# Attention on one core: the last weighted sums of a half issued together, and the copy of the sums two scores earlier

## The reference

```python
xn = layernorm(x)                                   # x: 8 x 1024 x 256
kqv = xn @ W_kqv.T                                  # 16 heads of 16 columns
score = einsum('bhsd,bhnd->bhsn', q, k) / 16 + slope[h] * (n - s)
attn = softmax(score, axis=-1)
out = einsum('bhsn,bhnd->bhsd', attn, v)
# routed experts: softmax of xn @ gate_w.T, the best 2 of 8, weights scaled by 2.5
y = sum over the two experts of combine * (silu(xn @ w_gate) * (xn @ w_up)) @ w_down
result = x + out + y + shared_expert(xn)
```

## Time and profile before

| | |
|---|---|
| median of three runs | 2621.71 us |
| the profiled execution | 2615.34 us |
| its span, first to last instruction | 2613.7 us |
| TensorE busy | 2438.0 us, 93% |
| VectorE busy | 1949.5 us, 75% |
| ScalarE busy | 1545.0 us, 59% |
| mean granted TensorE clock | 0.968 |

### The profile page before, as it was taken

How to read it: one execution, slowest core, us unless ns; L and a number is a source line. 1 busy time by engine, 2 the same in 40 slices (tenths; PEclk the granted TensorE clock), 3 DMA queues, 4 the chain that set the end, 5 groups by cost and what they waited for, 6 DMA issues and landing times.

```text
span 2613.7 us, 56931 instructions
## 1 busy us (share of the span) xinstructions
PE 2438.0 (93%) x19376; PEld 1487.8 (57%) x19377; DVE 1949.5 (75%) x2945; ACT 1545.0 (59%) x3215; POOL 790.3 (30%) x1004
## 2 busy tenths in 40 slices
PE   7999999963999999964999999999999999999998
PEld 5888888862999999861333333333333333333333
DVE  5666666643555555537899999999999999999994
ACT  3333333332333333320788888888888888888887
POOL 2222222235222222250101523505425135052250
PEclk9999999986999999985999999999999999999999
DMA  6999888740222222216324343534434353435330
GB/s 182 177 174 179 154 146 145 129 66 21 70 69 70 69 68 68 67 45 99 71 46 73 78 81 66 98 50 91 81 61 93 59 89 77 73 73 87 56 72 23
DMA packets 178264, 228.51 MB, mean 87 GB/s; under 512 B 43069, under 2 KB 127805, under 8 KB 178057
## 3 DMA queue, kind: packets, MB, share of 16 engines
q1 hardware_dynamic: 153336, 172.15, 36.7%
q0 software_dynamic: 22560, 50.69, 7.8%
q10 hardware_dynamic: 2176, 3.02, 0.3%
HBM read 131.60 MB, written 93.79 MB: 86 GB/s over the span
## 4 chain that ended last, share of the span: by engine, by line
PE 40%; DVE 13%; issue 1%; SPq 0%; DMA 0%; POOLq 0%; POOL 0%; ACT 0%; DVEq 0%
PE p_o L1358 17%; PE p L1348 15%; DVE part L1200 13%; PE p L1335 7%; PE p L1341 1%; DMA k_op<-ali_scratch 0%; POOLq L1113 0%; POOL q_op L1112 0%; SPq L1059 0%; ACT probs L1309 0%; SPq L1046 0%; PE p L1368 0%; ACT o_sb L1296 0%; DVE fin L1182 0%; DVE fin L1183 0%
## 5 line engine op out<-in xcount | busy, mean ns | idle before, releaser
L1200 DVE TENSOR_REDUCE part<-p 128x2 f32<-128x1024 f32 x1024 | 1248.8, 1225 | 95.8 <-PE p L1335 88.3
L1309 ACT ACTIVATE probs<-p 128x512 f32<-128x512 f32 x2048 | 1113.1, 597 | 232.0 <-PE p L1348 199.5
L1335 PE MATMUL p<-k_op,q_op 50*128 50x512 f32 x2048 | 759.5, 462 | 46.9 <-DMA k_op<-ali_scratch 36.6
L1348 PE MATMUL p<-q_op,k_op 51*128 51x512 f32 x2048 | 758.5, 451 | 25.9 <-DVE part L1200 25.9
L1358 PE MATMUL p_o<-probs,v_op 128*32 128x256 f32 x8192 | 656.2, 392 | 4.9 <-ACT o_sb L1296 0.8
L1348 PEld LDWEIGHTS p<-q_op,k_op 51*128 51x128 f32 x2048 | 316.4, 185 | 448.7 <-ACT probs L1309 369.5
L1358 PEld LDWEIGHTS p_o<-probs,v_op 128*32 128x32 f32 x8192 | 163.2, 108 | 338.1 <-ACT probs L1309 258.8
L1335 PEld LDWEIGHTS p<-k_op,q_op 50*128 50x128 f32 x2048 | 307.5, 189 | 61.9 <-issue 36.8
L763 POOL DMA_INDIRECT xe<-xn_scratch,ids x136 | 129.0, 948 | 393.0 <-DMA ids<-lists_scratch 386.4
L857 ACT CAST ht_hi<-pe_h 128x256 fp32r<-128x256 f32 x136 | 50.7, 373 | 289.8 <-PE pe_h L793 289.8
L1126 POOL DMA_DIRECT2D base_c<-base_scratch x56 | 32.2, 575 | 476.0 <-DVE att L1220 463.7
(11 more groups left out here) (177 smaller groups left out, 4137.2 us busy)
## 6 DMA issues: line engine op xcount, KB each, us to landing
qk_scratch<-qk_out SPq DMA_DIRECT2D x64, 512.0 KB
k_op<-qk_scratch SPq DMA_DIRECT2D x192, 128.0 KB
q_op<-qk_scratch SPq DMA_DIRECT2D x192, 128.0 KB
yr_scratch<-y SPq DMA_DIRECT2D x136, 128.0 KB, 1.7
v_scratch<-v_out SPq DMA_DIRECT2D x16, 1024.0 KB, 13.8
v_op<-v_scratch SPq DMA_DIRECT2D x32, 512.0 KB, 9.5
x<-in_x SPq DMA_DIRECT2D x16, 512.0 KB, 4.7
xn_scratch<-xn SPq DMA_DIRECT2D x16, 512.0 KB
```

Source lines behind the costliest of these rows:

```text
L1200: v.tensor_reduce(part[c_ % 2][:, kh, :, qb], p1[bank][:], AX.X, ALU.max, negate=True).then_inc(s["s1_read"], 1)
L1309: a.activation(probs[kb % 4][:, h], p2[bank2(u, r)][:], ACT.Exp).then_inc(s["s2_read"], 1)
L1335: return t.matmul(p1[bank][:, x], q_op[u][lo:lo + S1_ROWS, pair, q0:q0 + P], k_op[u][lo:lo + S1_ROWS, pair, kh * 512:(kh + 1) * 512], star ...
L1348: t.matmul(p2[bank][:], k_op[u][lo:lo + S2_ROWS, pair, kb * P:(kb + 1) * P], q_op[u][lo:lo + S2_ROWS, pair, half * HQ:(half + 1) * HQ], st ...
```

## The change

The last key block's side 1 is issued right behind its side 0, both at l = 1, and nothing is issued at l = 3. In every other key block the sides stay where they were, at the second and fourth unit. `OUT_COPY` goes from 3 to 1, so ScalarE's copy stands behind the exponential of l = 1. The number and kinds of instructions stay as they are.

```diff
@@ -996,7 +996,7 @@
         TURN_AT = {2 * CHUNK * c + 21: c for c in range(CHUNKS - 1)}
         OWN_TURN = 5
-        OUT_COPY, OUT_TURN = 3, 13
+        OUT_COPY, OUT_TURN = 1, 13
         OUT_ENTRY = (OUT_TURN + 1) // 2
@@ -1409,15 +1409,15 @@
-                    if l % 2 and (n > GH or has_prev):
-
-                        side = l % GH // 2
+                    if l % 2 and l != GH - 1 and (n > GH or has_prev):
+
                         k_ago = n // GH - 1
                         pe.wait_ge(s["s2_read"], b2 + 3 if k_ago < 0 else read[GH * k_ago + GH - 1])
-                        if k_ago < 0:
-                            products(g - 1, (u + 2) % 3, 1, NK - 1, side)
-                        else:
-                            products(g, u, k_ago // NK, k_ago % NK, side)
+                        for side in range(2) if l == 1 else [l % GH // 2]:
+                            if k_ago < 0:
+                                products(g - 1, (u + 2) % 3, 1, NK - 1, side)
+                            else:
+                                products(g, u, k_ago // NK, k_ago % NK, side)
```

## The result

The kernel after took 2640.86 us (median of six runs, 2635.47 to 2649.16), the kernel before, by then with six runs too, 2623.11 us (2620.36 to 2632.53). The ratio is 1.0063, with a 95% interval from 1.0036 to 1.0089: slower by more than the 0.2% that can be told apart. The way was as forecast; the size was +17.7 us between the medians where +10.0 were forecast, and 2640.86 lies above the range's upper end of 2636.0.

A forecast was written before the change was run, and what follows sets the result against it. TensorE was taken to pace the kernel, by its order within a half. +9.8 us over 61 halves and 0.2 in the last group made +10.0, so 2621.71 became 2631.7 us; range 2622.0 to 2636.0.

The forecast's parts named there:

- The bound, and the place that decides: At a half's boundary: TensorE paces, order within the half decides, and any delay of score 8 delays the whole half equally.
- The joined sides: Both sides at l = 1: 1.07 us together, TensorE saves 0.14 per half, score 2 at 1.67, score 4 at 2.35.
- The copy and exponential 3: On ScalarE: copy starts at 1.80, 0.06 behind the sides; exponential 3 ends at 3.38 instead of 2.87.
- The turn's wait: On TensorE behind score 5: turn's load 0.11 behind exponential 3's end, at 3.49; 0.05 was the cheap alternative.
- The sum of the regular part: Score 8 at 5.54 against 5.39: 0.16 us slower per half, +9.8 us over 61 halves.
- 0.2 in the last group: Last group, where ScalarE sets the pace: its two boundaries together cost 0.2 us.
- the clock stayed at 1.00: Rival 4: the change does not do what it says, only through a clock falling in the new gaps; chance 0.02.
- the turn's wait was not cheap: Rival 1: the turn's wait is cheap, 0.05, score 8 at about 5.46, +4.5 us in all, 2626.2 us; chance 0.17.
- VectorE's reductions: Rival 2: VectorE is the bound, reductions no closer than 1.24 us, new waits mostly covered, 2622 to 2624 us; chance 0.05.
- TensorE's savings stayed covered: Rival 3: TensorE's own order stays the bound, score 8 at 5.04, -0.35 per half, 2600.4 us; chance 0.09 with partial gains.
- the last of the sum and the range: Added +10.0 us to the runs' median 2621.71, giving 2631.7; upper end 2636.0 from +13 and a run's spread.

The follow-up runs named there:

- chip A: Chip of follow-up runs; kernels before and after rerun there without edit: 2614.92 and 2625.14 us, ratio 1.0029.
- chip C: Chip of follow-up runs; kernels before and after: 2630.00 and 2640.64 us; both without the gathers in seven of eight batches: 2625.37 and 2631.00 us.
- chip B: Chip of follow-up runs; kernel before 2630.12 us, kernel after, without edit, 2641.62 us; three further changed orders were profiled there.
- two changed orders: Kernel after with OUT_COPY back at 3: 2648.75 us, ratio 1.0106; kernel before with only OUT_COPY moved to 1: 2720.72 us, ratio 1.0351.

## Why the prediction was right, and where it was wrong

**The bound, and the place that decides.** Right. Whatever score 8 is late by reaches the end: the median from score 8 to the half's end is 16.000 us before and, on chip A, 16.000 after.

**The joined sides.** Right to 0.01: 1.07 us, and score 2 still 0.33 behind the last pass (1550.69 + 1.00 = 1551.69, of which three passes take 0.67). Score 4 stands at 2.29, inside the 2.22 to 2.35 that the prediction allowed, and it did not matter. By "TensorE: Matmul & The Clock Gate" of the Trainium skill, section "Step-by-step: what each phase is for", a load into the background buffer could have hidden there; this trace does not show it at a change from sums to scores.

**The copy and exponential 3.** Right. The copy starts at 1.81, 0.07 behind the sides' end at 1551.76. The same page of the Trainium skill, section "The cost: per-tile semaphore tail", gives for four tiles and one increment an estimate of 25 + 4.7 x 4 + 26.3 = 70 ns; the trace agrees.

**The turn's wait.** Right at 0.11 and not 0.05: by the trace exponential 3 lasts from 1552.80 to 1553.41, and the load is at 1553.52. Moving the turn took 0.086 us a half away.

**The sum of the regular part.** +0.16 was taken per half, +0.146 measured; over 61 halves 9.8 against 8.9, and 0.1 instead of 0.2 in the last group. Three chips give +10.2, +11.5 and +10.6 us between medians, against the forecast's +10.0. All three lie within 1.5 us of it, and the trace agrees step by step, so the mechanism was right and this is not luck. The rivals did not come: the clock stayed at 1.00 over the 61 halves, the turn's wait was not cheap, VectorE's reductions follow each other at 1.14 (1552.51 to 1553.65) and did not bind, and TensorE's savings stayed covered.

**The step that failed** is the last of the sum and the range: "on the median of the runs, 2621.71 + 10.0", with an upper end of "+13 and a run's spread". The mechanism held; the term that was mis-sized is the level. The prediction took the median of the three runs shown for the level on which the kernel after would be measured, and 2636.0 - 2621.71 - 13 = 1.3 us for a run's spread. The level itself moves: the three further runs of before taken for the comparison took 2621.89, 2629.87 and 2632.53 us, and the kernel before stands at 2614.92, 2630.12 and 2630.00 us on three chips. 2640.86 is 11.0 above the median of those three, 2629.87. That comparison was chosen after the fact, and whether those three runs met the same chip as the kernel after is not known. The first profile of the kernel after has late starts and the first of the kernel before has none, as if they came from different chips. There was no term for late starts, since the one profile shown had none, and they are 9 us over the 61 halves in the kernel before on chip C (1313.4 against 1304.3) and 13 us in the kernel after (1327.1 against 1314.0); in the first profile of the kernel after they are most of the 21.0 us behind score 8. By its own terms, +13 and 1.3, on a level of 2630.1 the range would have reached 2644.4.

**What stays open.** On chip C the late starts cost the kernel after 4 us more than the kernel before (13.1 against 9.1), by one profile each; whether the shifted order meets the gathers less well, or two executions just differ by that, was not settled. The timed +10.6 us on that chip holds about 9 us of the regular part, which leaves little for it, but the timed runs alone don't exclude a few microseconds. That POOL's gathers set off the late reports of TensorE is shown on chip C, where they were taken out; on chip B it rests on the late starts standing beside gathers there too. By what way they do it, and why chip A shows none with the same gathers, was not found.

## What to carry to other kernels

When an instruction is moved ahead of others on one engine, price it at the engine that waits for what it passed: here 0.14 us saved on TensorE and a wait of 0.12 us removed were outweighed, because the copy pushed exponentials 2 and 3 back by half a microsecond, and a ring of three banks makes score 5 and the turn wait for just these. One boundary worked out to 0.01 us from rows of one profile held on three chips; the absolute level did not, so add a forecast difference to a level only with the spread that several chips and executions show. With three engines all over 80% busy, as here, a piece of work can be cover for another engine: with the sides joined at l = 3 the same 0.14 us was saved, score 2 then waited 0.20 us for VectorE, and the time stayed the same.

## What the runs showed of the hardware that I had not expected

- On two of three chips, and in the first profile of the kernel after, TensorE raises its semaphores up to 1.6 us behind the modelled end of its rows, and the exponentials that start late by it all stand within 2.0 us behind the start of one of POOL's gathers: 40 to 58 times in an execution, 14.6 to 28.7 us in sum. ScalarE and VectorE wait meanwhile; all but two of the late exponentials, over all executions, start 0.02 us behind the semaphore. Without the gathers of `combine` it is two times and 0.6 us. What carries the delay was not measured.
- In the last group, where VectorE has no maxima to reduce, one execution each of two changed orders had TensorE's clock fall from 1.00 to 0.50 of full speed (2.4 to 1.2 GHz). In the case shown, TensorE had been busy for 9.25 us of the 10 us before the fall. The last group then took 60.8 and 67.3 us instead of 46.5. In all profiles of the kernels before and after, the clock stayed at 1.00 there up to the last 5 us.
- The end of the stretch at 0.50 in which the attention begins moves between executions, from 1245 to 1275 us, whatever the kernel, and with it the first half's time, from 31 to 39 us. That is 8 us of scatter between executions by itself.
- Durations overstate what an engine is occupied for: reductions of 1.23 us follow each other at 1.13, exponentials of 0.59 at 0.49.
